# Global attention in 64-column halves of TensorE's array, its trial scores in quarters

## The reference

```python
x = x + neighbourhood_attention(ln(x)); x = x + mlp(ln(x))     # 4 heads, 7 x 7 windows
t = to_tokens(x)                                                # (2, 1024, 64)
t = t + global_attention(ln(t))                                 # 8 heads of 64 channels
t = t + routed(ln(t))                                           # a scan over 33 steps, op picked by argmax
```

```python
q = (x @ Wq).reshape(b, t, h, e) * scale;  k, v likewise        # h = 8, e = 64, scale = e ** -0.25
att = softmax(einsum('bqhe,bkhe->bhqk', q, k))
out = einsum('bhqk,bkhe->bqhe', att, v).reshape(b, t, h * e) @ Wu + bu
```

## Time and profile before

| | |
|---|---|
| median of 3 runs | 647.61 us (645.7 to 652.51) |
| profiled execution, its own time | 652.3 us |
| its span | 650.5 us |
| granted TensorE clock, mean | 0.929 |
| TensorE matmuls busy | 574.0 us (88%), 3311 instructions |
| TensorE weight loads | 241.9 us, 3312 instructions |
| VectorE | 402.9 us (62%) |
| ScalarE | 316.0 us (49%) |
| GpSimd | 50.7 us (8%) |
| instructions in all | 8966 |

### The profile page before, as it was taken

The page is one execution under the profiler, slowest core; times in us unless marked ns, Lnnn a source line. Parts: engine busy times, 40 slices in busy tenths (PEclk is TensorE's granted clock), DMA queues, the critical chain, the costliest instruction groups (busy, mean ns, idle before and its releaser), DMA issues.

```text
span 650.5 us, 8966 instructions
## 1 busy us (share of the span) xinstructions
PE 574.0 (88%) x3311; PEld 241.9 (37%) x3312; DVE 402.9 (62%) x730; ACT 316.0 (49%) x460; POOL 50.7 (8%) x105
## 2 busy tenths in 40 slices
PE   6999998997499999999999999999999825599962
PEld 5554554554123234233333333233323211267611
DVE  5655546365775665867866776666552264798642
ACT  3645354834145584555555545555455323466330
POOL 6031133130110000100000010000000010000000
PEclk9999798968689999999999999999999958799976
DMA  4000000000000000000000000000000000000001
GB/s 107 1 2 2 1 2 1 1 2 1 1 0 1 0 1 1 2 0 2 0 1 1 0 2 1 1 8 0 1 1 0 1 4 2 13 1 2 1 0 33
DMA packets 9507, 3.22 MB, mean 5 GB/s; under 512 B 8820, under 2 KB 9079, under 8 KB 9463
## 3 DMA queue, kind: packets, MB, share of 16 engines
q1 hardware_dynamic: 8182, 2.61, 1.8%
q10 hardware_dynamic: 1281, 0.01, 0.1%
HBM read 2.09 MB, written 0.52 MB: 4 GB/s over the span
## 4 chain that ended last, share of the span: by engine, by line
PE 61%; issue 26%; DVE 8%; ACT 2%; POOL 1%; SPq 0%; DVEq 0%; POOLq 0%; DMA 0%; ACTq 0%
PE PS L779 11%; PE PS L756 10%; PE PS L741 4%; PE PS L666 4%; PE PS L680 4%; PE PS L693 3%; DVE most L1542 2%; PE PS L517 2%; PE PS L707 2%; PE PS L489 2%; PE PS L501 2%; PE PS L990 2%; PE PS L724 2%; PE PS L794 2%; PE PS L563 2%
## 5 line engine op out<-in xcount | busy, mean ns | idle before, releaser
L1542 DVE TENSOR_REDUCE most<-PS 128x2 f32<-128x1024 f32 x128 | 156.4, 1222 | 77.3 <-PE PS L741 77.0
L1191 ACT ACTIVATE PT<-PS 128x1024 f32<-128x1024 f32 x128 | 130.9, 1024 | 111.2 <-PE PS L756 110.6
L779 PE MATMUL PS<-PT,V 128*64 128x512 f32 x512 | 137.6, 617 | 0.0
L756 PE MATMUL PS<-qS,aS 128*128 128x512 f16 x512 | 133.1, 383 | 0.0
L756 PEld LDWEIGHTS PS<-qS,aS 128*128 128x128 f16 x512 | 44.9, 98 | 77.4 <-ACT PT L1191 21.1
L741 PE MATMUL PS<-aS,qS 64*128 64x512 f16 x128 | 51.0, 398 | 11.3 <-DVE most L1542 10.6
L1147 ACT ACTIVATE prob<-sbias,negm 128x320 f32<-128x320 f32 (+1 forms) x64 | 34.3, 537 | 45.4 <-DVE negm L1588 45.2
L741 PE MATMUL PS<-aH,qS 64*128 64x512 f16 x128 | 51.0, 398 | 0.0
L666 PE MATMUL PS<-ident 128*128 128x256 f16 x128 | 40.9, 320 | 7.3 <-DVE negm L1588 6.4
L1311 POOL TENSOR_TENSOR rstd<-var,minus_half 128x8 f32<-128x8 f32 x8 | 13.2, 1645 | 379.4 <-DVE var L1417 379.4
L336 DVE COPY PT<-PS 128x384 f32<-128x384 f32 (+1 forms) x32 | 16.7, 523 | 33.7 <-PE PS L693 33.7
(11 more groups left out here) (194 smaller groups left out, 709.0 us busy)
## 6 DMA issues: line engine op xcount, KB each, us to landing
xall<-in_x_dram SPq DMA_DIRECT2D x2, 256.0 KB, 4.4
out_dram<-x SPq DMA_DIRECT2D x4, 128.0 KB, 2.1
w<-in_L_attn_Wq_dram SPq DMA_DIRECT2D x2, 128.0 KB, 2.5
w<-in_L_attn_Wk_dram SPq DMA_DIRECT2D x2, 128.0 KB, 2.6
w<-in_L_attn_Wv_dram SPq DMA_DIRECT2D x2, 128.0 KB, 2.6
fc<-in_L_conv_fc_w_dram SPq DMA_DIRECT2D x2, 64.0 KB, 2.6
wu<-in_L_attn_Wu_dram SPq DMA_DIRECT2D x2, 64.0 KB, 2.4
w1s<-in_L_ffn_ffn_w_dram SPq DMA_DIRECT2D x2, 64.0 KB, 2.1
```

Of the source, the lines that this page charges most:

```text
L756: mm = pe.matmul(PS[:, score_banks(t) + lane, :], aS[:, k0:k0 + P], qS[:, part, lane, toks], start=(part == 0), stop=(part == 1))
L779: mm = pe.matmul(PS[cols, 6 + g % 2, :], V[:, img * NT + kt, cols], PT[:, g % 2, lane, kt, :], start=(kt == 0), stop=(kt == NT - 1))
L1191: act.activation(PT[:, g % 2, :, phase, :], PS[:, b0:b0 + 2, :], ACT.Exp).then_inc(c1["exped"], 1)
L1542: dve.tensor_reduce(most[:, g % 2, u // 2, u % 2, :], PS[:, 2:4, :], AX.X, ALU.max, negate=True)\
```

## The change

- `project`, `scores`, `head_outputs`: each product with 128 stationary columns becomes two with 64, the first into partitions 0 to 63 of the bank, the second into 64 to 127. Moving data and sums stay.
- `try_scores`: the same on top of the two halves of rows, so four products on four quarters of the array.
- `turn_shift`: the stationary operand is the shift column repeated 64 times instead of one column, so that 64 equal rows come out for each lane (one of them is read, as before); the lanes now alternate.

```diff
@@ project
                 for part in range(2):
-                    m = pe.matmul(bank, wqk[:, part, pair * 2 + lane, :, :].rearrange("p a c -> p (a c)"),
-                                  aS[:, blk * BLK:(blk + 1) * BLK], start=(part == 0), stop=(part == 1))
+                    for half in range(2):
+                        m = pe.matmul(bank[half * C:(half + 1) * C, :], wqk[:, part, pair * 2 + lane, half, :],
+                                      aS[:, blk * BLK:(blk + 1) * BLK], start=(part == 0), stop=(part == 1))
                 m.then_inc(piece_filled, 1)
@@ try_scores
-                    mm = pe.matmul(PS[:, 2 + lane, :], qS[rows, 0, lane, q0:q0 + P], keys[rows, k0:k0 + BLK],
-                                   start=True, stop=True)
+                    for h0 in (0, C):
+                        mm = pe.matmul(PS[h0:h0 + C, 2 + lane, :], qS[rows, 0, lane, q0 + h0:q0 + h0 + C],
+                                       keys[rows, k0:k0 + BLK], start=True, stop=True)
                 mm.then_inc(c1["tried"], 1)
@@ scores
                     for lane in range(2):
-                        mm = pe.matmul(PS[:, score_banks(t) + lane, :], aS[:, k0:k0 + P], qS[:, part, lane, toks],
-                                       start=(part == 0), stop=(part == 1))
+                        for h0 in (0, C):
+                            mm = pe.matmul(PS[h0:h0 + C, score_banks(t) + lane, :], aS[:, k0 + h0:k0 + h0 + C],
+                                           qS[:, part, lane, toks], start=(part == 0), stop=(part == 1))
                 mm.then_inc(c1["scored"], 1)
@@ head_outputs
-                    mm = pe.matmul(bank[:, j * 2 * (C + 1):(j + 1) * 2 * (C + 1)], OT[:, g % 2, q0:q0 + P],
-                                   wu1[:, pair, :, :].rearrange("p l c -> p (l c)"), start=True, stop=True)
+                    for h0 in (0, C):
+                        mm = pe.matmul(bank[h0:h0 + C, j * 2 * (C + 1):(j + 1) * 2 * (C + 1)],
+                                       OT[:, g % 2, q0 + h0:q0 + h0 + C],
+                                       wu1[:, pair, :, :].rearrange("p l c -> p (l c)"), start=True, stop=True)
                 mm.then_inc(c1["y_filled"], 1)
@@ turn_shift
-                for lane in range(2):
-                    for qt in range(QT):
-                        mm = pe.matmul(bank[C * lane:C * lane + 1, qt * P:(qt + 1) * P],
-                                       shift16[:, g % 2, lane, qt:qt + 1], ident16[:, :], start=True, stop=True)
+                for qt in range(QT):
+                    for lane in range(2):
+                        mm = pe.matmul(bank[C * lane:C * (lane + 1), qt * P:(qt + 1) * P],
+                                       shift16[:, g % 2, lane, qt:qt + 1].to_broadcast([P, C]), ident16[:, :],
+                                       start=True, stop=True)
                 mm.then_inc(shift_filled, 1)
```

## The result

The changed kernel took 631.03 us in the median (626.84 to 641.99, four runs) against 650.06 for the kernel before in the same comparison: ratio 0.969, interval 0.959 to 0.979. One of the four runs of the changed kernel (641.99 us, mean clock 0.911) counts as slow and is left out of the ratio. The profiled execution took 630.68 us, its span is 628.8.

What follows compares the result with a forecast made beforehand. TensorE was taken to bound the run from 183 to 504 us, nearly all the global attention. Gains and losses summed to -9.0 us, taking 647.6 to 638.6 us (chance 0.58), range 632.5 to 646.

Steps and rivals of the forecast that it cites:

- Trial scores (loss): Trial products in 117 global-attention steps: open first load and later starts cost 0.056 us each, +6.6 us.
- values to the next piece: Global-attention steps, from values to the following piece: stop and some load go, 0.11 us at 116 places, -12.8 us.
- head outputs to scores: Head outputs inside the steps: four f32 products become four pairs, 0.55 to 0.44 or 0.45, thirty times, -3.0 us.
- last 11 steps, beyond the above: Last steps without a trial: scores and values stay in one form, saving 0.155 us a step, -1.7 us.
- later half before the trial: Scores just before each trial: the second half starts 0.007 us later, +0.8 us.
- pieces left alone: Twelve unchanged extra pieces in steps: eight add 0.14 us each, four hidden-layer products 0.04 each, +1.3 us.
- Trial loads are quick: Rival in the trial scores: 64-column f16 loads as quick as 128, gain 14.0 us, 633.6 us; chance 0.13.
- the small end: Low price for trial scores: only +0.014 us a step, +1.6 us in all, if 64-column f16 loads are quick.
- the trials in turn with VectorE: Before 183 us: twelve early trials alternating with VectorE's maximum add 0.9 us, projection stops 0.3, total +1.2 us.
- Halves' weights in the open: Rival in scores, projection, head outputs: each of 684 pairs pays 0.05 us of load, 25 us slower, 673; chance 0.09.
- The stop is not one of form: Rival between scores and values: the stop has another cause and stays, 13.3 us of gain go, 652; chance 0.05.
- A part of the gain is lost: Rival: 3 to 8 us go again through pair costs or half-clock stretches, 641.5 to 647; chance 0.14.

Runs made afterwards that it cites:

- e6: Kernel before with only the change's trial scores in quarters added: 648.14 us, ratio 1.0068 to the kernel before.
- e2: Changed kernel with trial scores undone, two 128-column products on half the rows each: 638.78 us, ratio 0.973 to the kernel before.
- e5: Kernel before run again unchanged, one execution for its profile: 653.05 us.
- e1: Changed kernel run again unchanged, with more runs: 631.08 us, ratio 0.9719 to the kernel before.
- e8: Repeat of e4's version, trial scores on all 128 rows and 64 columns inside the steps: 625.03 us, ratio 0.9681 to the kernel before.
- e3: Changed kernel with the scores alone undone, four whole-array products in place of eight halves: 643.43 us, ratio 0.9902.
- e4: Changed kernel with trial scores from the twelfth on using all 128 rows and 64 columns: 624.36 us, ratio 0.9651 to the kernel before.
- e7: Changed kernel with the head outputs alone undone, four f32 products with 128 columns: 641.66 us, ratio 0.9971.

## Why the prediction was wrong

Inside the stage the mechanism was right, and one term was mis-sized. The step that failed is **Trial scores (loss)**: "The first product's load shows: 387 ns against 379 is 0.008 now; a first 64\*64 product is 267 against 218, 0.05", hence "+0.056 in 117 steps, +6.6 us". It cost 2.0 us.

Term by term, inside the stage. The measured column adds up the differences of all intervals between starts, before against after, from the first scores to the last values:

| term | predicted | measured |
|---|---|---|
| values to the next piece | -12.8 | 1.01 to 0.91 at 113 places, and 0.01 of load at 74: -12.2 |
| head outputs to scores | -3.0 | 0.55 to 0.44, 30 times: -3.2 |
| shift to scores | -1.4 | 0.33 to 0.22, 15 times: -1.6 |
| last 11 steps, beyond the above | -1.7 | 1.98 to 1.72: -1.6 |
| trial scores | +6.6 | 0.020 more behind them, 0.003 less ahead, in 117 steps: +2.0 |
| later half before the trial | +0.8 | 0.007 in 117 steps: +0.8 |
| pieces left alone | +1.3 | 0.09 more behind seven of them, 0.02 of open load behind all twelve: +0.9 |
| sum | -10.2 | -14.9; by the stage's ends -15.0 |

The prediction counted 116 places for the first term; the last three blocks of values already stood one behind the other. Its 0.007 for a second half's start stood on no row that it showed; it came out right. So the trials account for 4.6 of the 4.8 us by which the stage gained more than worked out. Taken off the 647.6 that the prediction started from, 15.0 gives 632.6, still just within the range. That the result lies below the range, 19.0 us apart instead of some 15, goes with what lies ahead of the stage, as set out below.

**The price of the load.** I took it from the only 64\*64 product in the trace, which is f32. The f16 load of the same 64 columns shows as 0.021 us, less than half of it. Against the 0.008 of before that is 0.013 more, where the prediction had 0.042; of the two later starts at 0.007, one shows (0.340 - 0.320 = 0.020 = 0.013 + 0.007). The trace of before had a hint that I passed over: an f32 product is issued as two instructions, so a row of that type need not give the price of an f16 one. e6 isolates the term: 335.2 to 337.3 is +2.1 us for 117 trials, and e2 takes 2.0 off again. The rival "Trial loads are quick" came nearest: +1.6 for the trials and 14.0 of gain in all.

The rule of the Trainium skill that the prediction cited ("TensorEngine Tiling (Array Packing)", Restrictions and Gotchas: column tiling disables Fast Weight Load) is not contradicted: 64 columns show as 0.021 where 128 show as 0.008. That section does not say how slow a load then is. I let an f32 row say it, and concluded that the small end was out; the runs came out near that end.

**The time ahead of the stage.** +1.2 us was predicted for the trials in turn with VectorE; from the first trial to the first scores the two profiles show 21.8 us (158.1 to 179.9) and 22.2 (150.2 to 172.4), so +0.4 (eleven trials lie there, not the twelve that were counted). The 7 to 8 us by which the whole part was earlier is no work saved. It goes with the half-clock stretches that fell into it. Each line below is the part up to the stage of one profile, in this order: before, e5, after, e6, e2.

```profile
0.00:182.00 182.00, 157.44 (x1100) 87.98 (x1101) 105.56 (x282) 80.84 (x160) 44.16 (x101) 0.88 0.05 11
0.00:183.00 183.00, 157.99 (x1100) 88.27 (x1101) 106.01 (x282) 80.98 (x160) 44.64 (x101) 0.89 0.05 11
0.00:175.00 175.00, 149.73 (x1142) 84.10 (x1145) 105.14 (x283) 81.12 (x160) 44.19 (x101) 0.94 0.05 11
0.00:175.50 175.50, 149.44 (x1125) 83.83 (x1127) 106.04 (x283) 81.38 (x160) 44.79 (x101) 0.94 0.05 11
0.00:190.00 190.00, 165.86 (x1118) 91.73 (x1121) 105.78 (x283) 81.61 (x160) 44.27 (x101) 0.84 0.04 10
```

The column before the last two is the clock: 0.88 and 0.89 in the two profiles of the kernel before, 0.94 in after and in e6, 0.84 in e2. From these means I estimate 44, 40, 21, 21 and 61 us at half clock in parts of 182, 183, 175, 175.5 and 190 us: the more half clock, the later the stage. VectorE's work in it is the same to 1%. e6 has the old stage and the early start, e2 the new stage and the latest start of all, so the start does not follow from the halves. The kernel before has both kinds of executions itself: of its 28 runs in the comparisons of e1 to e8, the 14 with a mean clock of 0.944 or more had spans of 639.1 to 644.6 us (median 643.4), while most of the others lay from 646 to 652. The changed kernel's five at such a clock had 624.9 to 629.3 (median 627.4). At equal clock the difference is 16.0 us, one more than the stage's 15.0. The 3 us by which the first comparison is above that are no more than the medians of the kernel before differ among themselves (645.25 to 650.06, below); the clocks of its runs before are not all on record, so this is not shown run by run. What decides where the stretches fall, and whether a kernel's own timing shifts the odds by the last us, stays open.

**The rivals.** "Halves' weights in the open" did not happen: eight half products take the 1.03 us of four whole ones, so pairs of scores follow every 0.216 us, and their loads ran under products in flight in the same rows of the array. "The stop is not one of form" is refuted by e3, where the stop comes back with the form. "A part of the gain is lost" did not happen either: the stage gained 15.0 us in both profiles of the changed kernel. VectorE stayed out of the way even in e4. What I got right by cause, the cadence of halves, was read from two blocks of f32 products; what I got wrong was read from one f32 block where the type mattered.

**What should have widened the range.** 632.5 was the quick-load case (633.6) with 1.1 us to spare. The kernel before alone has medians of 647.61 (three runs), 650.06 (four), 647.89 (17) and 645.25 (11), so the median of a few runs can by itself move the end by 2 or 3 us.

## What to carry to other kernels

Where TensorE is full, look at the form column (rows by columns of the array) along its own order of work: each change there cost about 0.10 us here beyond any load, whether the products on its two sides were both f16 or f16 and f32. It pays to bring neighbours to one form even if a product then streams twice as long: the trial scores on all rows were 5 us better than on quarters. Parts do not add: a single piece left in another form between two of the same costs two stops (e7: 10.2 us for 30 of them). Before you put a difference of a few us down to a change, read the stage that it enters between that stage's own ends. Take the price of a weight load from a row of the same type.

## What the runs showed of the hardware

- A load of 64 f16 columns ahead of the first product showed as 21 ns (400 against 379 ns, after), of 64 f32 columns as 50 (643 against 592 in the earlier trace rows); of 128 f16 columns on half the rows as 8 (387 against 379).
- A change of form stops the array for about 0.10 us, and for as long when rows and columns change at once (e3 and e6: whole array to quarters; e2: column halves to row halves) as when the rows alone do (before and after): scores to trial is 0.96 or 0.97 us in all of them.
- Two f16 halves side by side have the cadence of one whole product: eight took 1.03 to 1.04 us in after, four whole ones 1.03 to 1.04 in the earlier trace rows.
- A turned norm (L554, a transpose in f32) is listed as `128*64` like the values, and yet has a stop between itself and other `128*64` products on either side: 1.01 us behind the values instead of 0.91, and 0.56 to 0.59 to the scores, where it took 0.46 to 0.49 to the whole-array scores of before.
